# First attention scores as pairs of 64-row matmuls in six slots a step, with the turned maxima in a second-score bank

## The chip, the cores and the metric

The kernel runs on one core of a Trainium2 chip. Its time is the device time of one execution in microseconds (us); it is the median of several runs. The numbers of the profile come from one further execution that was recorded by the hardware profiler. Five engines work at once and meet only at semaphores: PE (TensorE, matmuls, with its weight loads shown apart as PEld), DVE (VectorE), ACT (ScalarE), POOL (GpSimd) and SP (SyncE, which here only issues DMAs).

## The reference, cut to what matters

The input is a batch of 8 sequences of 512 rows of 128 numbers. A modulated layer norm is followed by an attention block, its residual and a low-rank MLP, and then by a mixture of 8 experts with a shared expert. The change touches only the attention inside the first block:

```python
x = _layernorm(hidden_states, ln1_g, ln1_b)
Q = jnp.einsum('bsd,dhr,hre->bhse', x, q_U, q_V) + q_b[None, :, None, :]
K = ...
V = ...
scores = jnp.einsum('bhse,bhte->bhst', Q, K) * scale     # 16 heads of 8 numbers
scores = jnp.where(causal[None, None], scores, -1000000000.0)
attn = jax.nn.softmax(scores, axis=-1)
ctx = jnp.einsum('bhst,bhtd->bhsd', attn, V)
```

## The kernel before, in words

**What is multiplied.** A head has only 8 numbers a row, but they are wanted to near float32 precision. So Q and K are each split into three bf16 parts, and the six products of parts that matter (`PRODUCTS`) are stacked: 6 x 8 = 48 rows (`SROWS`) of contraction hold one head. Three more rows hold the negated maximum of each score row, again in three bf16 parts, against rows of ones on the side of K (`MROWS`, together `QROWS` = 51).

**Two passes over the scores.** The first scores (`s1`, L1232) have the queries on the partitions. DVE takes the maximum of each row of them (`take_max`, L1661, recorded at L1669). The second scores (`s2`, L1257) have the keys on the partitions and already contain the negated maximum, so ACT can take the exponential of them (`exp_unit`, L979, recorded at L989) and write the result where `context` (L1280, recorded at L1293) multiplies it with V. V has a column of ones, so that the sum of the exponentials comes with it.

**Steps and units.** A step handles one of 4 groups of 4 heads of one batch element: 32 steps (`NG`). In step n PE works on the second scores of n, on the context of n-1 and on the first scores of m = n+3. The first scores of a step are 12 units (`S1_UNITS`): two units for query tile 0 and two for query tile 1, each of two heads, and four units of one head each for tiles 2 and 3. The second scores are 6 units (`S2_UNITS`).

**How a unit is computed.** A first-score unit starts with one matmul of the causal mask (L1245, `ident_b` by `later_q`, over 128 rows), and then has one matmul a head (L1248). All of them contract over 128 partitions: `q_st` has a slice for each of the 4 heads in which the 64 partitions of the other half are zero, and `k_st` holds two heads above each other. The zeros are written once (ACT, L971, and two DMAs of zero rows in front, L534 to L538). A second-score unit works on 64-row halves instead: its two mask matmuls (L1272) and its score matmuls (L1276) alternate between partitions 0 to 63 and 64 to 127, each half with a PSUM bank of its own.

**The ring.** `ps_r` has three PSUM banks. `ring_order` (L115) lists everything that passes through them, in the order in which PE writes it: first-score units (S), the turned maxima (M), the transposed input (T), the projections Q, K and V, the output projection (O) and the transposed second norm (U). The entry at place k uses bank k mod 3, and `bank` (L1175) lets PE wait until the earlier entry in that bank has been read. `ps_s2` has four banks for the second scores, two for each unit in turn.

**The order on PE** (`step`, L1306): s2 units 0 and 1; context of key tile 0; s1 units 0 and 1; O; s1 2 and 3; s2 2 and 3; context of tiles 1 to 3; M; s1 4 and 5; T, K, V; s1 6 and 7; Q; s2 4 and 5; s1 8 to 11; U. T and Q come in one step of four, K and O in the next, V in the third and U in the fourth.

**The way of the maxima.** POOL splits the 16 maxima a row into bf16 parts (`split_max`, L825), PE turns them (`transpose_max`, L1252, recorded at L1254), ACT copies them to `max_rows` (`empty_max`, L1017, recorded at L1020), and SP stores them to DRAM (`store_max`, L592, recorded at L597) and loads them into the stack for the second scores two steps later (`load_max`, L599).

**Layer norms on DVE.** Between the maxima DVE does the norms of later and earlier batch elements: `layer_norm` (L1621) runs one half of a step's share after unit 3 and the other after unit 7. The batch elements' first norms end after about half of the steps; the second norms go on to the end.

**At the end.** In step 27 (`EARLY_STEP`) SP waits for several things and then issues the large loads for the MLP (L671 to L679); the loads and stores of the following steps stand behind them in its queue. `store_ctx` (L609) is one of these, and ACT's `empty_ctx` (L1022) waits for it two steps later.

Of the kernel before, what the change touches and what calls it, by code (L numbers as in the profile page):

```python
# [114 lines left out]
def ring_order():  # L115
# [12 lines left out]
    for n in range(FIRST_STEP, LAST_STEP + 1):  # L128
# [21 lines left out]
BY_ACT = {one: k for k, one in enumerate(one for one in RING if one[0] in "MTKVQU")}  # L150
# [95 lines left out]
def adaln_block(nc, a, out):  # L246

    ctx = ExitStack()
    with ctx:
# [6 lines left out]
        def sem(name):  # L256
            return ctx.enter_context(nc.semaphore(name))
# [35 lines left out]
        q_st = [first.take(GROUPS, JH, S, dt=BF16) for k in range(2)]  # L293
# [15 lines left out]
        q_d = dram("q_d", (2, len(PRODUCTS) + 1, P, S), BF16)  # L309
# [12 lines left out]
        def attend():  # L322
# [49 lines left out]
            later_q = sb("later_q", [P, P], BF16, until=front)  # L372
            ident_h = sb("ident_h", [P, HALF], BF16, until=front)
            lower_k = sb("lower_k", [P, P], BF16, until=front)
            upper_k = sb("upper_k", [P, P], BF16, until=front)
# [9 lines left out]
            consts, consts2, k_ones, v_ones, q_zeroed = sem("consts"), sem("consts2"), sem("k_ones"), sem("v_ones"), sem("q_zeroed")  # L385
# [8 lines left out]
            act_emptied, dve_emptied, zero_rows = sem("act_emptied"), sem("dve_emptied"), sem("zero_rows")  # L394
# [3 lines left out]
            max_split, max_stored, max_loaded = sem("max_split"), sem("max_stored"), [sem("max_loaded0"), sem("max_loaded1")]  # L398
# [6 lines left out]
            def ring(name, k):  # L405
                return ps_r[:, RING_BANK[PLACE[name, k]], :]

# [117 lines left out]
            with nc.Block() as block:  # L525
                @block.sync
                def _(sp):
# [6 lines left out]
                    sp.wait_ge(v_zeroed, 1)  # L534
                    for k in range(2):
                        sp.dma_start(q_d[k, len(PRODUCTS)].rearrange("p (c s) -> p c s", c=2),
                                     zeros[:].bitcast(BF16).unsqueeze(1).to_broadcast([P, 2, S // 2])).then_inc(zero_rows, 16)
# [14 lines left out]
                    def store_stack(b, m):  # L552
# [5 lines left out]
                        dst = (q_d, k_d)[m][b % 2, 0:len(PRODUCTS)].rearrange("k p s -> p k s")  # L558
# [11 lines left out]
                    def load_stack(b, g, of="qk"):  # L570
# [5 lines left out]
                        if b < 2:  # L576
                            wait(sp, k_ones, b + 1)
                            wait(sp, q_zeroed, b + 1)
                            wait(sp, zero_rows, 32)
# [1370 lines left out]
```

## Time and profile before

| | |
|---|---|
| median of 3 runs | 707.96 us (705.23 to 709.73) |
| the profiled execution | 706.39 us, of which the span from first to last instruction is 704.6 us |
| busy shares of the span | PE 90%, PEld 59%, DVE 64%, ACT 58%, POOL 43% |
| front part | first score matmul at 42.2 us |
| attention steps with first and second scores | 66 to 358 us |
| MLP, routing and experts | 382 us to the end |

"Busy" is the time in which at least one instruction of the engine was recorded as running. Matmuls overlap, and the end of a matmul is modelled, so a PE that is busy all the time may still be waiting for its own pipeline.

### The profile page before, as it was taken

To read this page: it belongs to the slowest core of one execution; us is meant where nothing else is said; L and a number is where in the kernel's file an instruction comes from. 1 tells how busy PE (TensorE), PEld (TensorE's weight loads), DVE (VectorE), ACT (ScalarE), POOL (GpSimd) and SP (SyncE) were. 2 spreads that over 40 slices of the span, in tenths; PEclk is the share of its full clock that TensorE was granted. 3 is DMA by queue.
4 is the path that set the end of the run, shared out by engine and by line. 5 is a ranking of instruction groups with operands and counts; after the bars stand their busy time and mean duration, and the time that the engine had idled before them with its cause. 6 is when DMAs were issued, how large, how long until landed. Compare 5 with 4: busy or idle time off the path is not lost.

```text
span 704.6 us, 15442 instructions
## 1 busy us (share of the span) xinstructions
PE 633.6 (90%) x5389; PEld 416.6 (59%) x5389; DVE 447.6 (64%) x1346; ACT 409.1 (58%) x720; POOL 301.7 (43%) x480
## 2 busy tenths in 40 slices
PE   4977899999999999999978886999998999999997
PEld 3543444444444544444434575766766999999993
DVE  5749887878788776767742878777673222222227
ACT  4432667676676767666666565676434555555550
POOL 4232424243442524232313438766771545455452
PEclk9999999999999999999999998999899999999999
DMA  9552332443343344332463511211236777777769
GB/s 212 189 177 74 118 102 87 144 138 113 109 153 102 126 140 136 131 106 72 132 189 108 143 36 50 81 51 50 70 96 197 205 239 222 221 224 225 234 209 322
DMA packets 86125, 100.97 MB, mean 143 GB/s; under 512 B 13008, under 2 KB 68216, under 8 KB 85952
## 3 DMA queue, kind: packets, MB, share of 16 engines
q1 hardware_dynamic: 76896, 87.19, 40.3%
q0 software_dynamic: 4544, 9.45, 3.7%
q10 hardware_dynamic: 4608, 3.35, 1.8%
q8 instruction: 43, 0.70, 0.4%
q14 instruction: 34, 0.28, 0.1%
HBM read 60.28 MB, written 37.57 MB: 139 GB/s over the span
## 4 chain that ended last, share of the span: by engine, by line
PE 53%; DVE 14%; DMA 9%; ACT 8%; SPq 6%; issue 5%; POOL 4%; POOLq 0%; ACTq 0%; DVEq 0%
PE ps_pv L1293 9%; PE ps_r L1478 7%; PE ps_s L1468 6%; DVE row_max L1669 6%; PE ps_r L1248 5%; PE ps_r L1245 4%; DMA arena<-slots_d 4%; PE ps_pv L1364 4%; PE ps_s L1276 3%; POOL slots_d L910 3%; PE ps_r L1223 2%; PE ps_s L1272 2%; PE ps_s L1372 2%; ACT arena L1081 2%; DMA arena<-in_w_mod 1%
## 5 line engine op out<-in xcount | busy, mean ns | idle before, releaser
L1669 DVE TENSOR_REDUCE row_max<-ps_r 128x1 f32<-128x384 f32 (+3 forms) x384 | 206.9, 595 | 63.1 <-PE ps_r L1248 61.8
L989 ACT ACTIVATE arena<-ps_s 128x1024 f32<-128x1024 f32 (+1 forms) x192 | 159.3, 881 | 70.8 <-PE ps_s L1276 69.8
L1248 PE MATMUL ps_r<-arena 128*128 128x384 bf16 (+3 forms) x512 | 118.7, 303 | 0.0
L956 POOL DMA_INDIRECT y_d<-arena,target x78 | 74.9, 960 | 87.7 <-DVE arena L1878 75.5
L1245 PE MATMUL ps_r<-later_q,ident_b 128*128 128x128 bf16 (+1 forms) x384 | 91.4, 244 | 22.0 <-DVE row_max L1669 15.8
L1245 PEld LDWEIGHTS ps_r<-later_q,ident_b 128*128 128x128 bf16 x384 | 35.9, 97 | 84.1 <-DVE row_max L1669 42.4
L1874 DVE TENSOR_TENSOR arena<-ps_r,arena_early 128x256 f32<-128x256 f32 x39 | 16.6, 425 | 108.2 <-PE ps_r L1478 108.2
L1293 PE MATMUL ps_pv<-arena 128*32 128x512 f32 (+3 forms) x1024 | 83.3, 443 | 0.1
L910 POOL DMA_INDIRECT slots_d<-arena,slots x64 | 65.5, 1023 | 18.2 <-issue 18.2
L1276 PE MATMUL ps_s<-arena 51*128 51x256 bf16 (+3 forms) x512 | 59.9, 298 | 0.0
L1478 PEld LDWEIGHTS ps_r<-arena 128*128 128x128 f32 x480 | 58.2, 192 | 1.5
L1144 ACT ACTIVATE arena<-ps_s,arena 128x256 f32<-128x256 f32 x120 | 50.4, 471 | 13.9 <-PE ps_s L1468 13.2
L1478 PE MATMUL ps_r<-arena 128*128 128x128 f32 x480 | 58.3, 275 | 0.0
L1248 PEld LDWEIGHTS ps_r<-arena 128*128 128x128 bf16 x512 | 50.6, 99 | 12.8 <-issue 2.4
L1468 PE MATMUL ps_s<-arena 128*128 128x256 f32 x240 | 56.8, 379 | 0.0
L831 POOL TENSOR_SCALAR neg_part<-row_max 128x16 bf16<-128x16 f32 x32 | 8.3, 260 | 89.0 <-DVE row_max L1669 89.0
L1293 PEld LDWEIGHTS ps_pv<-arena 128*32 128x32 f32 x1024 | 27.0, 110 | 32.2 <-issue 25.8
L1468 PEld LDWEIGHTS ps_s<-arena 128*128 128x128 f32 x240 | 43.3, 190 | 4.6
L1272 PE MATMUL ps_s<-ident_h,lower_k 64*128 64x64 bf16 (+1 forms) x384 | 39.9, 204 | 5.2 <-ACT arena L989 4.7
L1102 ACT ACTIVATE arena<-ps_s,cols 128x512 f32<-128x512 f32 x32 | 21.6, 686 | 31.6 <-PE ps_s L1372 30.9
L770 POOL TENSOR_TENSOR var_eps<-moments,ln_eps 128x4 f32<-128x4 f32 x24 | 4.9, 203 | 79.9 <-DVE moments L1494 79.9
L1272 PE MATMUL ps_s<-ident_h,upper_k 64*128 64x64 bf16 (+1 forms) x384 | 38.7, 198 | 0.0
(236 smaller groups left out, 1129.1 us busy)
## 6 DMA issues: line engine op xcount, KB each, us to landing
arena<-in_ew SPq DMA_DIRECT2D x30, 514.0 KB
ctx_d<-ctx_raw SPq DMA_DIRECT2D x32, 256.0 KB, 3.1
arena<-q_d SPq DMA_DIRECT2D x64, 102.0 KB
arena<-k_d SPq DMA_DIRECT2D x64, 96.0 KB
arena<-slots_d SPq DMA_DIRECT2D x39, 132.0 KB, 3.1
arena_early<-in_ew SPq DMA_DIRECT2D x9, 514.0 KB
arena<-y_d SPq DMA_DIRECT2D x8, 512.0 KB, 6.0
q_d<-arena_early SPq DMA_DIRECT2D x8, 384.0 KB, 2.9
```

Of the source, the lines that this page charges most:

```text
L910: pool.indirect_dma_start(slots_d[:], bass.IndirectOffsetOnAxis(ap=slots[:, c, i:i + 1], axis=0), n3x[:, c, i, :], None).then_inc(scattere ...
L956: pool.indirect_dma_start(y_d[:], bass.IndirectOffsetOnAxis(ap=target[:, k, c:c + 1], axis=0), res[:, k, c, :], None).then_inc(put[k], 16)
L989: act.activation(dst, src, ACT.Exp, scale=SCALE).then_inc(exp_done, 1)
L1144: act.activation(x_hidden[:, k, f], ps_s2[:, 2 * (k % 2) + f // 2, (f % 2) * SLOTS:(f % 2 + 1) * SLOTS], ACT.Relu, bias=x_w[k][:, FF + NF ...
L1245: pe.matmul(diag, ident_b[:], later_q[:].unsqueeze(1).to_broadcast([P, len(js), P]), start=True, stop=False, skip_group_check=True)
L1248: mm = pe.matmul(bnk[:, k * keys:(k + 1) * keys], q_st[b % 2][:, g, j, i * P:(i + 1) * P], k_st[b % 2][:, g, j // 2, 0:keys], start=False, ...
L1272: pe.matmul(banks[half][:, :, at:at + HALF], stationary[whole], near, start=(at == 0), stop=False, skip_group_check=True)
L1276: mm = pe.matmul(banks[j % 2][:, k // 2, :], k_st[b % 2][rows, g, j // 2, kt * P:(kt + 1) * P], q_st[b % 2][rows, g, j, kt * P:S], start=F ...
L1293: mm = pe.matmul(ps_pv[32 * j:32 * j + 32, kt * P:S], v_sb[b % 2][:, kt, GROUPS * j + g, :], probs[:, p % 2, at:at + length], start=(kt == ...
L1468: mm = pe.matmul(ps_s2[:, 2 * (k % 2) + f // 2, (f % 2) * SLOTS:(f % 2 + 1) * SLOTS], x_w[k][:, f * P:(f + 1) * P], tok_t[:, k], start=Tru ...
L1478: mm = pe.matmul(ps_s1[:, k % 2, c * P:(c + 1) * P], x_hidden[:, k, f, c * P:(c + 1) * P], x_w[k][:, FF + f * D:FF + (f + 1) * D], start=( ...
L1669: dve.reduce_max(row_max[:, m % 2, js[0] % 2, j:j + len(js), i], src, AXIS.X).then_inc(max_taken, 1)
```

## The change

The first scores are computed like the second ones. `q_st` loses the zero halves (two slices a group, not four), and a pair of units, one for each 64-row half, is written together into two ring banks: first the mask matmuls of both halves, two to a half (`lower_q`, `upper_q`, 64 columns a head each), then the score matmuls, alternating between the halves. PE waits for both banks before it starts the pair. The zero rows, their DMAs and ACT's two fills of `q_st` go. The order of the step is written anew in six slots, each with one pair of first-score units and one second-score unit; the context is cut into four, O moves behind the second half of the step. The turned maxima leave the ring: they are written to columns 384 to 447 of bank 3 of `ps_s2`, which only second-score unit 1 uses. ACT still copies them behind the exponential of unit 3, which itself comes later in the step, and units 1 and 5 of the second scores wait for that copy. DVE's norms are cut into quarters, after units 1, 3, 7 and 9.

```diff
@@ ring_order
-        units(m, 0, 1)
-        one(n, "O")
-        units(m, 2, 3)
-        if 0 <= m - 1 < NG:
-            order.append(("M", m - 1))
-        units(m, 4, 5)
-        one(n, "T", "K", "V")
+        units(m, 0, 1, 2, 3, 4, 5)
+        one(n, "T", "K")
         units(m, 6, 7)
+        one(n, "O", "V")
+        units(m, 8, 9)
         one(n, "Q")
-        units(m, 8, 9, 10, 11)
+        units(m, 10, 11)
@@ s1
-        for u in units:
+        for u in units[::2]:
...
+            banks = [bank("S", NS1 * m + u + half)[:, 0:len(js) * keys].rearrange(...) for half in range(2)]
+            for stationary, at in ((lower_q, keys - P), (upper_q, keys - HALF)):
+                for half in range(2):
+                    whole = slice(HALF * half, HALF * half + HALF)
+                    near = ident_h[whole].unsqueeze(1).to_broadcast([HALF, len(js), HALF])
+                    pe.matmul(banks[half][:, :, at:at + HALF], stationary[whole], near, start=(at == keys - P), stop=False, ...)
             for k, j in enumerate(js):
+                for half in range(2):
+                    rows = slice(HALF * half, HALF * half + SROWS)
+                    mm = pe.matmul(banks[half][:, k, :], q_st[b % 2][rows, g, j // 2, i * P:(i + 1) * P],
+                                   k_st[b % 2][rows, g, j // 2, 0:keys], start=False, stop=True, ...)
+                    if k == len(js) - 1:
+                        mm.then_inc(s1_done, 1)
@@ transpose_max
         pe.wait_ge(max_split, SPLIT_OPS * (m + 1))
+        wait(pe, max_copied, m)
+        wait(pe, exp_done, NS2 * n + 2)
+        pe.transpose(max_turned(), ...)
@@ s2
+        if u == 1:
+            wait(pe, max_copied, min(n + LAG - 1, NG))
+        if u == 5:
+            wait(pe, max_copied, min(n + LAG, NG))
@@ step on PE, new order
+        s1(m, 0, 1)
         s2(n, 0)
+        context(n - 1, 0)
+        s1(m, 2, 3)
         s2(n, 1)
+        context(n - 1, 1)
+        s1(m, 4, 5)
         s2(n, 2)
+        context(n - 1, 2)
+        context(n - 1, 3)
         (T, K where due)
+        s1(m, 6, 7)
+        transpose_max(n)
+        s2(n, 3)
+        (O, V where due)
+        s1(m, 8, 9)
+        s2(n, 4)
         (Q where due)
+        s1(m, 10, 11)
+        s2(n, 5)
         (U where due)
@@ step on ACT
         exp_unit(n, 2)
-        exp_unit(n, 3)
-        empty_max(n + LAG - 1)
         empty_ctx(n - 1)
-        qk_middle(b, 0)
         empty_t, empty_qk(b, 1)
+        exp_unit(n, 3)
+        empty_max(n + LAG - 1)
         empty_v
+        qk_middle(b, 0)
+        exp_unit(n, 4)
         empty_qk(.., 0)
-        exp_unit(n, 4)
         exp_unit(n, 5)
@@ layer_norm on DVE
-        second = u == 7
+        second = u > 4
+        quarters = {1: (0, 1), 3: (2, 3), 7: (0, 1), 9: (2, 3)}[u]
```

The masks on POOL become two tensors of 192 columns instead of three of 128.

## Rows read from the trace of the kernel before

**Rows 1.** The page: the chain that ended last, by engine.

```profile
PE 53%; DVE 14%; DMA 9%; ACT 8%; SPq 6%; issue 5%; POOL 4%; POOLq 0%; ACTq 0%; DVEq 0%
```

**Rows 2.** Windows of four steps, an early and a late batch: busy us, clock, DMA.

```profile
172.30:213.77 41.47, 38.60 (x434) 19.48 (x432) 34.16 (x90) 28.28 (x42) 16.70 (x33) 1.00 0.38 128
...
255.22:296.70 41.48, 39.11 (x438) 19.70 (x436) 29.75 (x64) 28.68 (x42) 14.24 (x29) 1.00 0.38 128
```

**Rows 3.** Chain of waits, first-score units: start us, us, what.

```profile
98.46 0.11 PE ps_r L1245
98.57 0.11 PE ps_r L1248 x2
...
98.79 0.22 PE ps_r L1248 x2
...
101.96 0.06 PE ps_r L1245
102.01 0.16 PE ps_r L1248
...
105.86 0.22 PE ps_r L1248
```

**Rows 4.** Chain of waits, second-score units on 64-row halves.

```profile
96.86 0.06 PE ps_s L1272 x4
96.92 0.22 PE ps_s L1276 x2
...
99.81 0.06 PE ps_s L1272 x4
99.87 0.16 PE ps_s L1276 x2
...
104.98 0.22 PE ps_s L1276 x4
105.21 0.11 PE ps_s L1272 x4
105.32 0.11 PE ps_s L1276 x4
```

**Rows 5.** Chain of waits, what else PE does in a step.

```profile
97.13 0.99 PE ps_pv L1293 x8
...
100.03 1.43 PE ps_pv L1293 x24
...
102.17 0.55 PE ps_r L1209 x4
...
103.67 1.10 PE ps_r L1223 x2
```

**Rows 6.** Timeline of DVE and PE: start us, us, instruction, idle before it.

```profile
231.34 0.76 DVE L1669 TENSOR_REDUCE row_max<-ps_r 128x2 f32<-128x256 f32 x2 [1.01 <-PE ps_r L1248]
...
231.36 1.11 PE L1303 MATMUL ps_r<-w_out,ctx_n 128*128 128x128 f32 x8
...
232.83 1.29 DVE L1669 TENSOR_REDUCE row_max<-ps_r 128x2 f32<-128x512 f32 x2 [0.74 <-PE ps_r L1248]
...
245.38 1.02 DVE L1669 TENSOR_REDUCE row_max<-ps_r 128x1 f32<-128x384 f32 x2 [0.26 <-PE ps_r L1248]
...
251.72 1.96 DVE L1669 TENSOR_REDUCE row_max<-ps_r 128x2 f32<-128x256 f32 x4 [0.73 <-PE ps_r L1248]
```

**Rows 7.** Chain of waits behind step 27: SP's queue and a store.

```profile
348.42 5.38 SPq L673
...
358.45 4.73 DMA ctx_d<-ctx_raw
```

**Rows 8.** Windows of 2 us in the first steps: busy us, granted clock.

```profile
52.00:54.00 2.00, 0.90 (x6) 0.42 (x6) 1.93 (x9) 0.00 (x0) 1.04 (x4) 1.00 0.00 1
...
56.00:58.00 2.00, 1.94 (x9) 0.83 (x9) 1.85 (x5) 0.00 (x0) 0.00 (x0) 0.50 0.41 139
...
60.00:62.00 2.00, 1.33 (x11) 0.63 (x9) 2.00 (x6) 0.00 (x0) 0.90 (x4) 1.00 0.19 67
```

**Rows 9.** Timeline of ACT in the front part, behind its fills of the stacks.

```profile
21.57 0.78 ACT L996 ACTIVATE arena_early<-ps_r,cols 128x512 f32<-128x512 f32 x1 [8.43 <-PE ps_r L1209]
```

More of the change, by code:

```diff
@@ L289, in adaln_block @@
         work = first.take(2 * PT_LEN)
-        q_st = [first.take(GROUPS, JH, S, dt=BF16) for k in range(2)]
+        q_st = [first.take(GROUPS, 2, S, dt=BF16) for k in range(2)]
+        first.at += GROUPS * 2 * S
         k_st = [first.take(GROUPS, 2, S, dt=BF16) for k in range(2)]
@@ L606, in load_max @@
                             row = HALF * half + SROWS
[L607 removed]
+                            sp.dma_start(q_st[b % 2][row:row + MROWS, g], src[:, half]).then_inc(max_loaded[m % 2], 16)
                     def store_ctx(p):
@@ L1252, in transpose_max @@
-                    def transpose_max(m):
+                            banks = [bank("S", NS1 * m + u + half)[:, 0:len(js) * keys].rearrange("p (j s) -> p j s", s=keys) for half in range(2)]
+                            for stationary, at in ((lower_q, keys - P), (upper_q, keys - HALF)):
+                                for half in range(2):
+                                    whole = slice(HALF * half, HALF * half + HALF)
+                                    near = ident_h[whole].unsqueeze(1).to_broadcast([HALF, len(js), HALF])
+                                    pe.matmul(banks[half][:, :, at:at + HALF], stationary[whole], near, start=(at == keys - P), stop=False,
+                                              skip_group_check=True)
@@ L1632, in layer_norm @@
                         if b is not None:
-                            for i in range(NT):
+                            for i in quarters:
                                 if second:
@@ L1639, in layer_norm @@
                         if b is not None:
-                            for i in range(NT):
+                            for i in quarters:
                                 if second:
@@ L1646, in layer_norm @@
                         if b is not None:
-                            for i in (2, 3) if second else (0, 1):
-                                normalise(b, i)
+                            normalise(b, quarters[0] // 2 + 2 * second)
                         b = batch_at(n, AFTER_STATS_AT)
                         if b is not None:
-                            for i in range(NT):
+                            for i in quarters:
                                 if second:
@@ L1657, in layer_norm @@
                         if b is not None:
-                            for i in (2, 3) if second else (0, 1):
-                                normalise_after(b, i)
+                            normalise_after(b, quarters[0] // 2 + 2 * second)
                     def take_max(m, u):
```

109 lines of the change are left out of this document (43 added, 66 removed).

## The prediction

> **What bounds the kernel now.** I read the chain by engine first: PE carries 53% of it and DVE 14% [rows 1], so the end is set by PE with DVE in between. Then the windows of four steps. In the attention a batch of four steps takes 41.47 us with PE busy 38.60, DVE 34.16 and ACT 28.28; in a late batch, when the first norms are over, the length is the same with DVE at 29.75 [rows 2]. So PE is nearly full, and DVE is second with 7.3 us of idle time a batch (41.47 - 34.16), 11.7 late. Last the timeline: DVE's waits, 0.3 to 1.0 us each, are for first scores [rows 6]. They come because PE goes off for second scores and context (0.99 us for key tile 0, 1.43 us for the rest [rows 5]) while the ring holds only three units of DVE work. The change touches both: it takes work from PE, and it spreads first-score units over the step.
>
> **PE's saving.** A first-score unit costs, by its pitch in the chain: tile 0: 0.11 + 0.11 = 0.22; tile 1: 0.11 + 0.22 = 0.33; tile 2: 0.06 + 0.16 = 0.22; tile 3: 0.06 + 0.22 = 0.28 [rows 3]. A step has 2, 2, 4 and 4 of them: 0.44 + 0.66 + 0.88 + 1.12 = 3.1 us. A new pair has the form of a present second-score unit, column for column: four masks of 64 columns in 0.06 and two matmuls of 512 in 0.22 or of 384 in 0.16; four masks of 128 in 0.11, four matmuls of 128 in 0.11 or of 256 in 0.22 [rows 4]. So a pair costs 0.22, 0.33, 0.22 or 0.28, and a step has 1, 1, 2, 2 of these: 1.55 us. Saved: 1.55 us a step, 6.2 a batch. Changes between array shapes: context of tile 0 takes 0.99 us [rows 5] for 4 x 512 columns in 0.85, so a change costs about 0.1; plain steps have eight both before and after, and O, V and Q now sit between 64-row neighbours, 0.6 us more a batch. PE's work a batch falls from about 38.6 to 33 busy, or 31.3 by pitch: four plain steps of 6.3 (below) and 6.1 for projections and transposes (T 0.55, U alike, K, Q, V, O 1.1 each [rows 5, 6], with their changes of shape).
>
> **What DVE then allows.** DVE's work does not shrink. In pairs the maxima cost 0.76 (tile 0), 1.29 (512 columns) or 1.02 (384) [rows 6]: 0.76 + 1.29 + 2 x 1.02 + 2 x 1.29 = 6.67 us a step, 26.7 a batch. Today four tile-0 and tile-1 units run on in 1.96 [rows 6], slightly better than 2.05; the groups broken up cost 1.0 a batch in all. The rest of 34.16 is 8.5 us of norms. New floor by DVE: 35.2 us a batch, 30.7 late. Both floors lie far under 41.5; what counts is how the two engines mesh. I go slot by slot. A pair needs two of three banks, so PE may start it when DVE has taken the first unit of the pair before, and needs about 0.05 for the semaphore, 0.17 for the pipeline to fill, and the pair itself. Between two deliveries PE has:
> - to slot 2 (tile 1): second-score unit, context 0, change, pair: 0.28 + 0.99 + 0.11 + 0.33 = 1.71 us;
> - to slot 3: 0.28 + 0.75 + 0.11 + 0.22 = 1.36; to slot 4: 0.22 + 0.75 + 0.11 + 0.22 = 1.30; to slot 5: M 0.27, 0.33, 0.28 = 0.88; to slot 6: 0.61; to the next slot 1: 0.44 (together 6.3).
> DVE has 0.76, 1.29, 1.02, 1.02, 1.29, 1.29 there and a quarter of the norms after slots 1, 2, 4 and 5. In an early batch (norm quarters of 0.3 to 0.7) DVE idles:
> - step with V: slot 2 comes 0.16 late, V (1.1) makes slot 5 0.25 late: 0.4;
> - step with U: 0.1; U itself fits while PE waits, but as an odd entry in a ring of three it makes the next pair wait for both units before it: the next step loses 0.4 there and 0.4 at slot 2, and T (0.55) makes slot 4 0.5 late: 1.3;
> - step with K and O: 0.44 at slot 2, 1.1 at slot 4 (K before the pair), and 0.65 in which DVE waits for O itself: 2.2.
> Sum 4.1, so a batch takes 35.2 + 4.1 = 39.3, a gain of 2.1 us. In a late batch the same slots with smaller quarters idle 1.3 + 0.5 + 2.8 + 2.7 = 7.3: 30.7 + 7.3 = 38.0, a gain of 3.5. There are some 4.5 early and 2.5 late batches with both kinds of scores: 9.5 + 8.7 = 18.2 us.
>
> **A rule on evacuation, and one on modes.** The row shows DVE busy 34.16 of 41.47 us [rows 2] before PE gets any faster. The Trainium skill (TensorEngine Tiling (Array Packing), PSUM Bottleneck) says that tiling speeds up the matmuls but not the reading of PSUM, which may become the bottleneck; it speaks against counting PE's 6.2 us a batch as the gain. By the rule at its strictest a batch would be DVE's 35.2; by the slots it is 39.3. The same page (Key Properties) has a change of tiling mode drain the array; the 0.1 us in the context's 0.99 [rows 5] agrees.
>
> **What is moved, and its price.**
> - The turned maxima. Counted from the step's second-score unit 0, they are turned about 4.8 us into a step today (four second-score units 1.1, context 0.99 + 1.43, four first-score units 1.1, M 0.17 [rows 3 to 5]). Now M stands as late after slot 1 (1.71 + 1.36 + 1.30 and its own 0.3), and ACT copies behind the exponential of unit 3 (0.8, with 0.3 of matmuls and 0.3 of latency): 1.2 us later. Behind it in ACT's queue stand V's emptying, a cast and exponential 4, which has over 1 us of slack, and in SP's queue `store_ctx` and the loads of later stacks, which have a step or more. In the middle this costs nothing: the maxima are wanted more than a step later, and the new waits of units 1 and 5 are for a copy long done or 1 us old. If a step's cover is gone, each costs the 1.2 us. It does cost once: in step 27 SP's long loads stand behind `load_max`; one of them is held 5.38 us, and ACT then waits for a store of 4.73 us [rows 7]. That chain starts with M of step 27, so gains behind it are lost (left out of the 7 batches above) and the 1.2 us is paid. Lower end 0 (SP is held by something else), upper end 3.
> - The clock. In the first steps, before second scores begin, PE waits for DVE already. The clock fell to its lower level, 1.2 GHz (0.50 in 56 to 58 us), after PE had been busy 0.90 of 2 us; with 1.33 of 2 us it held [rows 8]. With half the work in the first scores those steps (some 25 us) will run at the lower level. A pair then takes 0.44 to 0.66, more than DVE's second unit leaves, 0.15 us in each of 18 slots: 2.5 us lost. Lower end 0, upper end 5.
> - The front part: two fills on ACT and two DMAs fewer. ACT idles 8.43 us behind its fills before the first transposed input comes [rows 9], so they are hidden and their going brings nothing; at most 1 us through lighter DMA. The masks on POOL are 7 + 6 instructions instead of 9 + 7, with about as many elements; they are hidden behind PE's 6.9 us of small products. Loads of `q_st` move 48 rows instead of 51: nothing.
>
> **Sum.** 706.4 (span 704.6 and 1.8 around it) - 18.2 + 1.2 + 2.5 = 691.9 us. The median of the runs shown is 1.6 us above the profiled execution, so I forecast 693.5 us.
>
> **The rivals.**
> 1. DVE becomes the one bound and the slots mesh better than I think. For it: DVE's waits need only 0.3 us more of lead at slot 2. Against it: K, O and T still stand ahead of a pair. If half of the idle time I count (2 us early, 3.6 late) goes, 4.5 x 2 + 2.5 x 3.6 = 18 us more: 676.
> 2. The mesh is no better than now: pairs need two banks of three, and DVE keeps its 7.3 us of idle a batch on a work 1.0 us larger: 42.5 early. Late, with 10 idle, 40.7. That is 4.5 x 1.0 - 2.5 x 0.8 = +2.5, and 3.7 for maxima and clock: 714; halfway between this and my forecast, 704. For it: three banks, PE blocked in order. Against it: waits today come from runs of four units ahead of 2.4 us of other work, which the slots end.
> 3. The clock falls inside the steps (other side). Between slot 4 and the next slot 1 PE has 1.9 us of work in 4.3 us of DVE's. With filled pipelines that shows as about 65% busy, near the 1.33 of 2 that held, above the 0.90 that fell [rows 8]. If it falls, the work there is hidden, but context 0 and slots 2 and 3 run at half speed: 1.71 + 1.36 = 3.1 us more. In one step of four, seven times, that is 22 us: 715. It decides from five such falls on (15 us); in every step it would be over 760.
> 4. The halves don't run side by side, so the change doesn't do what it says: PE stays at 3.1 us a step and only the order changes, with 0.6 us a batch for changes of shape and the 3.7: 706.4 + 4.2 + 3.7 + 1.6 = 716. Against it stand the second scores, where two 512-column matmuls take 0.22 [rows 4].
>
> **How the numbers follow.** Chances: forecast 0.55, rival 1 0.13, rival 2 0.18, rival 3 0.12, rival 4 0.02. The forecast's own range is 684 to 701 (costs at their ends, and 1 us a batch either way). The range for 8 in 10 leaves out about half of rival 1 and most of rival 3: 677 to 709. A measurement of this kernel can tell about 1%, 7 us, from no change. Faster by over 1% (below 701): forecast nearly whole and rival 1: 0.67. Within 1%: 0.18, rival 2 above all. Slower: 0.15, from rivals 3, 2 and 4.
>
> **What would show it.** In the profile after: L1245's and L1248's successors with twice the matmuls and some 1.5 us less of pitch a step; a window of four early steps of about 39.3 us with DVE busy near 35 and PE near 33; DVE's longest waits at slot 4 of the K step and at O; the clock at 0.5 between 50 and 70 us and at 1.00 from the first second scores on; SP's 5.38 us stall still there, and the wait after it as long or longer. Wrong would be: a batch of 41 us or more (meshing), one under 37 (rival 1), a clock under 0.95 in the steady windows (rival 3), or second-score units waiting for ACT's copy of the maxima.

## The result and the profile after

The changed kernel takes 726.27 us (median of 4 runs, 724.77 to 730.82) against 708.17 us of the kernel before, run beside it (4 runs, 705.23 to 709.73): ratio 1.0271, 95% interval 1.0215 to 1.0328. It is slower; the forecast of 693.5 us and its range, 677 to 709, are missed, on the far side. One further execution, of 738.74 us, was in a slower state and is left out. The profiled execution took 730.82 us with a span of 729.1; that of before took 706.39, 24.4 us less.

The page of the kernel after: busy times, granted clock by slices, and the chain by engine.

```profile
PE 605.4 (83%) x5773; PEld 391.1 (54%) x5773; DVE 450.6 (62%) x1346; ACT 411.5 (56%) x718; POOL 301.5 (41%) x478
...
PEclk9855599999998798999997999899999999999999
...
PE 50%; DVE 15%; DMA 12%; SPq 8%; ACT 7%; issue 5%; POOL 3%; ACTq 0%; POOLq 0%; DVEq 0%
```

PE's share of the chain falls from 53% to 50% [rows 1], so the change took work from the engine that bounded the kernel, and the time went up all the same. The three fives in the clock row are the first steps; in two later slices it stands at 7.

To see where, I cut both attention parts at the start of the first maximum of every fourth step (m = 0, 4, ..., 28) and at the end of the last maximum: the window's length is then DVE's own pitch, and doesn't depend on where a marker stands in PE's order. Windows of the kernel before, then of the kernel after (length, busy us of PE, PEld, DVE, ACT, POOL, granted clock, DMA share, GB/s):

```profile
42.66:79.76 37.10, 27.67 (x194) 13.15 (x193) 31.80 (x74) 14.56 (x23) 12.86 (x27) 0.91 0.38 125
79.76:119.08 39.32, 37.14 (x423) 17.96 (x422) 32.04 (x84) 27.65 (x41) 14.22 (x31) 1.00 0.32 105
119.08:158.99 39.91, 37.98 (x431) 18.99 (x430) 32.01 (x78) 27.59 (x41) 14.24 (x30) 1.00 0.37 125
158.99:200.44 41.45, 38.58 (x435) 19.48 (x434) 34.16 (x91) 28.25 (x42) 16.70 (x34) 1.00 0.38 126
200.44:241.88 41.44, 38.57 (x435) 19.45 (x434) 34.07 (x90) 28.25 (x42) 16.68 (x33) 1.00 0.38 128
241.88:283.06 41.18, 38.58 (x435) 19.47 (x434) 29.96 (x66) 28.25 (x42) 14.24 (x29) 1.00 0.39 128
283.06:321.29 38.23, 35.90 (x427) 18.50 (x426) 28.82 (x63) 24.14 (x35) 10.82 (x27) 1.00 0.34 117
321.29:358.30 37.01, 34.87 (x421) 18.03 (x419) 28.72 (x63) 23.39 (x34) 9.21 (x23) 1.00 0.42 129
```

```profile
43.33:85.42 42.09, 25.79 (x225) 11.95 (x225) 32.56 (x74) 12.71 (x21) 11.97 (x24) 0.58 0.31 98
85.42:125.08 39.66, 33.77 (x474) 15.33 (x468) 32.07 (x84) 28.10 (x39) 12.45 (x29) 0.93 0.25 80
125.08:168.53 43.45, 35.20 (x482) 16.55 (x476) 32.13 (x79) 29.31 (x41) 15.63 (x33) 0.92 0.38 123
168.53:210.39 41.86, 32.87 (x485) 16.08 (x480) 34.11 (x92) 29.52 (x42) 16.81 (x34) 1.00 0.38 125
210.39:260.08 49.69, 39.85 (x485) 17.80 (x480) 36.38 (x91) 29.62 (x42) 16.76 (x34) 0.83 0.33 105
260.08:303.27 43.19, 35.26 (x485) 16.61 (x480) 30.36 (x68) 29.50 (x42) 14.57 (x30) 0.92 0.37 120
303.27:341.86 38.59, 31.43 (x477) 15.32 (x472) 29.30 (x64) 25.54 (x35) 10.80 (x26) 0.96 0.41 134
341.86:378.52 36.66, 30.64 (x477) 14.87 (x472) 29.23 (x64) 25.89 (x35) 9.73 (x25) 1.00 0.36 106
```

The differences are +5.0, +0.3, +3.5, +0.4, +8.2, +2.0, +0.4 and -0.4 us, 19.6 in all; 0.7 us had been lost ahead of them. From the last maximum to the last addition of an output projection it takes 43.9 us before and 49.1 after; the MLP and the experts behind it take what they took (302.4 and 301.5 us).

Two things can be read here. In the one early batch that stands wholly at clock 1.00 (41.86 us), PE's busy time did fall, from 38.6 to 32.9, but PE idles 9.0 us (2.9 before) and DVE 7.8 (7.3 before): the time that PE won became waiting. That batch is 0.4 us longer than before and 2.6 us longer than the forecast's 39.3, with no help from the clock. And the batches that lose more are those with a low clock. The granted clock has two levels, 1.2 and 2.4 GHz, so 43.45 us at 0.92, 49.69 at 0.83 and 43.19 at 0.92 hold about 7, 17 and 7 us at the lower one. At half speed PE's work there can be late by half of that at most, 3.5, 8.5 and 3.5 us (an estimate); lost against before are 3.5, 8.2 and 2.0.

The pairs themselves do what the change says. The chain of after, near step 28 (start us, us, what):

```profile
352.12 0.22 PE ps_r L1240 x4
352.34 0.22 PE ps_r L1245 x4
...
353.62 0.16 PE ps_r L1240 x4
353.78 0.17 PE ps_r L1245 x2
```

A pair's score matmuls, four of 256 columns or two of 384, take 0.22 and 0.17 us; that is the forecast's price from [rows 4]. The masks ahead of them, 0.22 and 0.16, hold the 0.1 us for the change of shape behind the context. Rival 4 is out.

The waits inside the batch at full clock, 168.53 to 210.39 us, and the first one behind it. Timeline of DVE in the kernel after (in brackets: idle before, and what ended it), and two rows of PE from the same stretch:

```profile
187.13 0.55 DVE L1699 RECIPROCAL recs<-sums 128x64 f32<-128x64 f32 x1 [0.81 <-DMA sums<-ctx_d]
...
191.37 1.29 DVE L1676 TENSOR_REDUCE row_max<-ps_r 128x2 f32<-128x512 f32 x2 [1.31 <-PE ps_r L1245]
...
204.82 1.02 DVE L1676 TENSOR_REDUCE row_max<-ps_r 128x1 f32<-128x384 f32 x2 [1.19 <-PE ps_r L1245]
207.07 0.69 DVE L1692 TENSOR_TENSOR h_sb<-ps_r,h_sb 128x512 f32<-128x512 f32 x1 [1.23 <-PE ps_r L1310]
...
213.40 1.29 DVE L1676 TENSOR_REDUCE row_max<-ps_r 128x2 f32<-128x512 f32 x2 [1.61 <-PE ps_r L1245]
```

```profile
190.83 0.28 PE L1240 MATMUL ps_r<-ident_h,later_q 64*128 64x128 bf16 x4 [0.79 <-ACT after_t L1021]
...
205.91 1.13 PE L1310 MATMUL ps_r<-w_out,ctx_n 128*128 128x128 f32 x8 [0.62 <-ACT arena_early L996]
```

Row by row: the wait for the sums of the probabilities, whose load stands behind the stack loads in SP's queue; slot 2 behind U, where PE waits until ACT, busy with the first exponential, has emptied U; slot 4 behind K, the 1.1 us of the forecast; O, which PE can't start before ACT has emptied K's bank; and slot 2 again in a step where the clock is low. Windows of 2 us around that fall:

```profile
208.00:210.00 2.00, 0.71 (x16) 0.56 (x18) 2.00 (x6) 1.46 (x3) 1.92 (x4) 1.00 0.36 126
210.00:212.00 2.00, 2.00 (x22) 0.54 (x22) 1.79 (x6) 1.50 (x2) 1.67 (x5) 0.60 1.08 391
212.00:214.00 2.00, 2.00 (x22) 0.86 (x22) 0.60 (x1) 0.06 (x1) 1.37 (x2) 0.54 0.10 26
```

PE had waited for DVE, busy 0.71 of 2 us, and then the clock stands at its lower level, 1.2 GHz, for about 3.4 us in these two windows. The context of key tile 0, 0.99 us [rows 5], takes 1.93 there. This is rival 3's picture. Counted over the trace between 100 and 360 us, the clock is low for 34 us, where before it was low for none. What this costs the kernel as a whole is less certain: the experiments below raise the clock and win little.

The end: from the chain of after, and then PE's wait there in the timeline of before and of after:

```profile
371.26 4.87 SPq L669
...
381.32 5.11 DMA ctx_d<-ctx_raw
...
389.72 1.86 PE ps_pv L1300 x8
```

```profile
364.92 0.20 PE L1272 MATMUL ps_s<-ident_h,lower_k 64*128 64x64 bf16 x2 [2.83 <-ACT arena L989]
```

```profile
388.10 0.40 PE L1279 MATMUL ps_s<-ident_h,later_k 64*128 64x128 bf16 x4 [6.28 <-ACT max_rows L1011]
```

SP's stall and ACT's wait for a store are still there, about as long as in [rows 7]. But in the new order of ACT exponential 3 and the copy of the maxima stand behind `empty_ctx`, which is what waits for that store, and second-score unit 5 waits for the copy: PE stands for 6.28 us where it stood for 2.83. This is the one place where second scores wait long for the copy, a sign of being wrong that the prediction named. The context behind it runs at the low clock. I did not test this part by itself.

### The profile page after: what moved, and what is told of

The parts are those of the page before. It is cut to its first block, busy times and chain, and to the rows that moved or that the text cites. A ratio compares the mean times of both kernels' runs of the same rounds, so it can differ in the third digit from the quotient of the medians.

```text
span 729.1 us, 16417 instructions
## 1 busy us (share of the span) xinstructions
PE 605.4 (83%) x5773; PEld 391.1 (54%) x5773; DVE 450.6 (62%) x1346; ACT 411.5 (56%) x718; POOL 301.5 (41%) x478
## 3 DMA queue, kind: packets, MB, share of 16 engines
q1 hardware_dynamic: 76608, 86.53, 39.7%
## 4 chain that ended last, share of the span: by engine, by line
PE 50%; DVE 15%; DMA 12%; SPq 8%; ACT 7%; issue 5%; POOL 3%; ACTq 0%; POOLq 0%; DVEq 0%
PE ps_pv L1300 9%; DVE row_max L1676 8%; PE ps_r L1486 7%; PE ps_s L1476 7%; PE ps_r L1240 4%; PE ps_pv L1372 4%; PE ps_r L1245 3%; DMA arena<-slots_d 3%; POOL slots_d L904 3%; PE ps_s L1283 3%; DMA k_d<-arena_early 2%; DMA arena<-y_d 2%; PE ps_r L1216 2%; PE ps_s L1380 2%; SPq L585 2%
## 5 line engine op out<-in xcount | busy, mean ns | idle before, releaser
L1676 DVE TENSOR_REDUCE row_max<-ps_r 128x1 f32<-128x384 f32 (+3 forms) x384 | 212.0, 594 | 67.2 <-PE ps_r L1245 65.0
L980 ACT ACTIVATE arena<-ps_s 128x1024 f32<-128x1024 f32 (+1 forms) x192 | 168.3, 882 | 96.6 <-PE ps_s L1283 94.3
L1240 PEld LDWEIGHTS ps_r<-ident_h,later_q 64*128 64x128 bf16 x768 | 25.3, 96 | 156.4 <-DVE row_max L1676 78.3
L1240 PE MATMUL ps_r<-ident_h,later_q 64*128 64x64 bf16 (+1 forms) x768 | 51.3, 212 | 67.3 <-DVE row_max L1676 63.5
L1300 PE MATMUL ps_pv<-arena 128*32 128x512 f32 (+3 forms) x1024 | 99.3, 487 | 0.0
L1245 PE MATMUL ps_r<-arena 48*128 48x384 bf16 (+3 forms) x512 | 75.6, 329 | 0.0
L904 POOL DMA_INDIRECT slots_d<-arena,slots x64 | 66.1, 1034 | 18.2 <-issue 17.9
L1283 PE MATMUL ps_s<-arena 51*128 51x256 bf16 (+3 forms) x512 | 72.3, 315 | 0.0
L1279 PE MATMUL ps_s<-ident_h,later_k 64*128 64x64 bf16 (+1 forms) x768 | 49.9, 206 | 8.1 <-ACT max_rows L1011 6.3
L1279 PEld LDWEIGHTS ps_s<-ident_h,later_k 64*128 64x128 bf16 x768 | 37.1, 100 | 26.8 <-ACT arena L980 12.5
L851 POOL TENSOR_TENSOR ctx_n<-ctx_t,rec_rows 128x512 f32<-128x512 f32 x8 | 10.4, 1298 | 60.7 <-DMA rec_rows<-rec_d 60.6
```

Of the source, the lines that this page charges most:

```text
L904: pool.indirect_dma_start(slots_d[:], bass.IndirectOffsetOnAxis(ap=slots[:, c, i:i + 1], axis=0), n3x[:, c, i, :], None).then_inc(scattere ...
L980: act.activation(dst, src, ACT.Exp, scale=SCALE).then_inc(exp_done, 1)
L1240: pe.matmul(banks[half][:, :, at:at + HALF], stationary[whole], near, start=(at == keys - P), stop=False, skip_group_check=True)
L1245: mm = pe.matmul(banks[half][:, k, :], q_st[b % 2][rows, g, j // 2, i * P:(i + 1) * P], k_st[b % 2][rows, g, j // 2, 0:keys], start=False, ...
L1279: pe.matmul(banks[half][:, :, at:at + HALF], stationary[whole], near, start=(at == 0), stop=False, skip_group_check=True)
L1283: mm = pe.matmul(banks[j % 2][:, k // 2, :], k_st[b % 2][rows, g, j // 2, kt * P:(kt + 1) * P], q_st[b % 2][rows, g, j // 2, kt * P:S], st ...
```

## The experiments

Each kernel was timed beside runs of the kernel before on the same chip. On the chips used the kernel before takes 708 to 724 us, so only ratios are compared. The chips differ behind the attention: in the traces of the changed kernel on two of them (after and after_again) the last addition of an output projection ends at 427.6 and 428.6 us, and what follows takes 301.5 and 318.2. The sixteen kernels went in four groups.

### First group: the two halves of the change, filler, and two waits

**order_only**: the new order, the cut norms and the free corner, with the first scores as before.

```diff
-banks = [bank("S", ...) for half in range(2)]   # masks and scores, alternating
+bnk = bank("S", n)                               # one mask over 128 rows, then the scores
```

> The new order of the step, ACT's and DVE's new orders and the turned maxima in the corner, but first scores as before: one unit at a time over 128 rows. Mesh theory (the new order and the single entries in a ring of three cost the time): about as slow as the change or slower, 720 to 735, since PE has 1.55 us more a step and the same waits behind O, U and T. Clock theory (the time is lost because half-empty PE lets the clock fall): PE keeps its columns, the granted clock stays at 0.97 or more in the span, and the time comes back to 705 to 713.

Measured: ratio 1.0516 (1.0449 to 1.0583), clock 0.951: slower than either theory had it.

**pairs_only**: pairs in the old order, the maxima in the ring.

> First scores in pairs of 64-row halves, in the old order of the step with the maxima in the ring. Mesh theory: the pairs alone do little harm, since the singles stand where they stood: 700 to 712. Clock theory: PE has the same few columns as in the change, so the clock falls in the first steps and now and then later (0.92 to 0.96 over the span), and the time is 715 to 728.

Measured: 1.0500 (1.0432 to 1.0568), clock 0.914. Again slower than either theory had it. Neither half is a gain: each alone costs 5%, both together 2.5 to 2.7%. That the order needs the time that the pairs free is my reading of this; which waits make the pairs in the old order slow was not traced down (its clock is low for 51 us between 100 and 360).

**fill_steps**: the change, with idle mask rounds ahead of the second scores, so that PE has more to do. Each round is started and then overwritten by the unit's own masks.

```diff
+FILL_S2 = {3: 4, 4: 6, 5: 8}
+for _ in range(FILL_S2.get(u, 0)):
+    for half in range(2):
+        pe.matmul(banks[half][:, :, 0:HALF], lower_k[half], near, start=True, stop=False)
```

> The change, with 18 further rounds of mask matmuls a step ahead of second-score units 3, 4 and 5 (0.85 us of PE at the full clock), which are overwritten by the real masks: work that brings nothing but fills PE where it waits for DVE. Clock theory: from the first second scores on the clock is back at 0.98 to 1.00, and the time falls by 4 to 12 us, to 714 to 722. Mesh theory: PE waits there anyway, so the time stays within 3 us of the change's 726, or rises.

Measured: 1.0245 (1.0177 to 1.0313), about the changed kernel's own ratio (1.0271, and 1.0251 in the second group; it was not run on this chip). The low clock between 100 and 360 us fell from 34 to 14 us, and the median did not follow: 4 to 12 us were expected of the clock.

**singles**: the change, with O and V behind units 8 and 9 (slot 6; ACT empties V behind exponential 4), and U emptied at the end of its own step.

```diff
-one(n, "O", "V")
 units(m, 8, 9)
+one(n, "O", "V")
...
-exp_unit(n, 0); empty_after(...)      # first thing of the next step
+qk_middle(b, 1); empty_after(...)     # end of the same step
```

> The change, with O and V moved one slot on, between the second-score unit 4 and the last pair, where DVE has most to do, and the transposed second norm (U) emptied by ACT at the end of its own step instead of behind the first exponential of the next. Mesh theory: DVE's waits at O (1.2 us) and behind U (0.8 to 1.3 us) go, some 2 us a batch, 12 to 16 us in all: 710 to 716. Clock theory: little, 722 to 727.

Measured: 1.0196 (1.0110 to 1.0283). Of the 12 to 16 us expected some 4 came, within the intervals. The waits for O went (in the traces 6.0 us in all before the edit, 0.2 with it), those for the sums did not (6.6 and 8.4 us).

### Second group: the waits mended, and filler everywhere

**after_again** is the changed kernel itself on the second group's chip.

> The changed kernel itself, beside the following ones on the same chip: 1.027 times the time of before if the first measurement carries over; the granted clock low for some 25 to 30 us in the first steps and for 30 to 50 us later.

Measured: 1.0251 (1.0189 to 1.0313), the first measurement over again.

**fill_all**: as fill_steps, with 22 rounds a step, and 512-column matmuls ahead of each pair in the first three steps.

> The change, with idle matmuls in both places where PE waits for DVE: two of 512 columns ahead of each pair in the three steps before the second scores, and 22 rounds of mask matmuls a step ahead of second-score units 3, 4 and 5. Clock theory: the low clock in the first steps (some 30 us) and later (34 us of the attention) goes, and 8 to 14 us come back: ratio 1.008 to 1.016. Mesh theory: little of it comes back, ratio 1.02 to 1.03, since DVE idles behind ACT, the sums and O and not for PE's work.

Measured: 1.0175 (1.0104 to 1.0245), clock 0.953: between the two theories, and its interval overlaps that of after_again.

**waits**: singles, and the loads of the sums ahead of the loads of the stacks in SP's queue.

```diff
+load_ctx(batch_at(n, CTX_AT))
 for g, later in ((0, 0), (1, 0), (2, 1), (3, 2)):
     ...                               # loads of the stacks
-load_ctx(batch_at(n, CTX_AT))
```

> The change with three waits moved away: O and V one slot later, U emptied by ACT at the end of its own step, and the loads of the sums ahead of the stacks in SP's queue. No filler. Mesh theory: DVE's waits at O (1.2 us) and for the sums (1.3 us) go, 2.5 us a batch, 15 to 18 us in all: ratio near 1.005. Clock theory: PE's idle stretches stay as long, the clock falls as often or oftener, and the ratio stays between 1.015 and 1.03.

Measured: 1.0069 (1.0030 to 1.0108). The three lone waits together (O and V, U, the sums) were worth 1.8%, some 13 us, the largest part of the loss that an experiment isolates. The clock stayed: between 100 and 360 us it is low for 31 us in this trace, against 34 in after.

**waits_fill**: both.

> Both at once. If the two causes add up, 20 to 28 us come back: ratio 0.985 to 1.0. If the clock alone counts, as in fill_all. If neither is the cause, near 1.025.

Measured: 1.0058 (1.0026 to 1.0090); the 0.985 to 1.0 did not come. In the trace the filler does what the clock theory says; a batch of waits, and one of waits_fill:

```profile
168.83:213.20 44.37, 35.83 (x485) 16.71 (x480) 36.64 (x91) 29.51 (x42) 16.86 (x33) 0.92 0.35 118
```

```profile
163.72:203.98 40.26, 36.67 (x661) 19.85 (x656) 34.47 (x92) 29.28 (x42) 16.71 (x34) 1.00 0.40 130
```

4.1 us less in the same order, with the clock at 1.00. (The first of them holds some 7 us at the lower level, which can make PE's work late by 3.5 us at most, so not all of the 4.1 need be the clock.) But the medians are 728.40 and 727.08: filler in the whole kernel gives 0.1%, within its interval nothing. It takes PE's time itself, and falls of the clock remain elsewhere (a batch of 44.29 us at 0.92). So the low clock is real and goes with longer batches, but filler doesn't buy the time back.

### Third group: is it the coupling of the two banks?

A pair asks for two of three banks, and delivers both its units together. **apart** is waits with the two 64-row units of a pair issued one after the other, each behind its own bank, wherever the entry ahead of the pair is T, K, V, O, Q or U; **apart_all** does so for all pairs.

```diff
-banks = [bank("S", k0 + half) for half in range(2)]
-for ... in masks:  for half in range(2): pe.matmul(...)
-for k, j in ...:   for half in range(2): pe.matmul(...)
+for half in range(2):
+    banks[half] = bank("S", k0 + half)
+    for ... in masks: pe.matmul(...)
+    for k, j in ...:  pe.matmul(...)
```

> The kernel waits with one edit: where the ring's entry just ahead of a pair of first-score units belongs to T, K, V, O, Q or U (six pairs a batch of 24), the two 64-row units are issued one after the other, each behind its own bank, instead of interleaved behind both banks. Theory of the coupled banks (a pair asks for two of three banks at once, so behind a lone entry VectorE has nothing left to take while TensorE makes the pair): VectorE's idle time ahead of such pairs falls by some 0.3 to 0.5 us a time, 2 to 3 us a batch at most, and the ratio to the kernel before goes from waits' 1.007 to 0.990 to 1.000. Rival: the halves one after the other take longer, and the late unit is what decides; then it stays at 1.005 to 1.015, with VectorE idle only moved from the first unit of the pair to the second. Third theory, the clock: nothing here fills TensorE, so a ratio of 1.005 whatever the idle time inside.

Measured: 1.0029 (1.0002 to 1.0056), between the first theory's range and the others'.

> As apart, but all six pairs of a step are issued one unit after the other: 64-row units with nothing side by side, in the new order, with the waits mended. It measures what the side-by-side halves are worth in this order. By the forecast's price of the pairing (1.55 us of matrix work saved a step, some of it idle anyway) it is slower than waits by 0.5 to 1 us a step where TensorE's queue decides: ratio 1.02 to 1.04. If the pair's coupling costs as much as it saves, it equals waits, 1.00 to 1.012.

Measured: 0.9938 (0.9911 to 0.9964), 703.90 us against 708.19. Giving up the side-by-side issue altogether, for which the change was made, makes this kernel faster than the kernel before. The expectation of 1.02 to 1.04 failed outright.

**before_sums** is the kernel before with the loads of the sums first.

> The kernel before with one edit: the loads of the sums of probabilities go ahead of the loads of the stacks in the queue of SyncE, as in waits. In the kernel before the wait for the sums is 0.44 us a batch, so by the theory that this wait was the change's own harm it gives at most 0.5 us a batch, 3 us in all: ratio 0.996 to 1.000. If it gives 1 per cent or more, the sums' place was a fault of both kernels, and what waits won by it doesn't speak of the change.

Measured: 1.0039 (1.0013 to 1.0066). In the old order that edit is a small loss, a little outside the expected range (in the trace of before the waits for the sums are 0.43, 0.89, 0, 0.81 and 0.29 us), so the sums' place is no fault of both kernels.

**apart_fill**: apart, with the filler of waits_fill.

> apart with the idle matrix work of waits_fill (two 512-column matmuls ahead of each pair in the first three steps, 22 rounds of masks a step ahead of the second scores 3 to 5). If the clock is what remains once the waits are gone, the ratio is 0.985 to 0.995 and below apart's by 0.005 or more; if the filler costs as much as the clock gives back, as it did for waits, the ratio equals apart's within 0.004.

Measured: 1.0000 (0.9977 to 1.0024), so the filler costs about what it gives back. Its profile is the cleanest of the new order. A batch, then DVE's waits in it:

```profile
198.70:238.38 39.68, 37.02 (x661) 20.15 (x656) 34.39 (x92) 29.43 (x42) 16.66 (x34) 1.00 0.41 132
```

```profile
222.93 1.02 DVE L1690 TENSOR_REDUCE row_max<-ps_r 128x1 f32<-128x384 f32 x2 [0.57 <-PE ps_r L1254]
...
233.15 1.02 DVE L1690 TENSOR_REDUCE row_max<-ps_r 128x1 f32<-128x384 f32 x2 [1.18 <-PE ps_r L1254]
...
236.39 0.69 DVE L1706 TENSOR_TENSOR h_sb<-ps_r,h_sb 128x512 f32<-128x512 f32 x1 [0.47 <-PE ps_r L1324]
```

39.7 us a batch, 1.8 below the 41.45 of before. The forecast had 39.3, with 0.5 at slot 4 behind T, 1.1 behind K and 0.65 at O. Where the clock holds and the lone entries are out of the way, the slot-by-slot sum was right to 0.4 us for an early batch. Some of that is luck: DVE is busy for 34.4 and idle for 5.3 us, where the forecast had 35.2 and 4.1, and the two errors cancel.

### Fourth group: the change as it stands, and the order without halves

**after_apart**: the changed kernel, nothing mended, with the pairs issued apart.

> The changed kernel with one edit: the two 64-row units of a pair are issued one after the other, each behind its own bank. Nothing else is undone: the order, the loads, the masks by halves and the free corner stay. Theory of the coupled banks: the interleaving costs about as much here as it did with the mended waits (1.003 or 1.007 to 0.994, some 1 per cent), so the ratio falls from 1.025 to 1.010 to 1.018. Rival: TensorE's queue decides in this kernel because its waits stand in it, so the lost side-by-side time (some 1.5 us a step of matrix work by the forecast) comes back in full where it isn't idle; then 1.025 or more.

Measured: 1.0159 (1.0106 to 1.0212). The interleaving costs about 0.9% here (against after_again, measured on another chip; the intervals touch).

**apart_all_fill**: apart_all with the filler.

> apart_all with the idle matrix work of waits_fill (512-column matmuls ahead of the first-score units in the first three steps, 22 rounds of masks a step ahead of the second scores 3 to 5). apart_all still shows 31 us at the low clock between 100 and 360 us. If the clock is what is left, the ratio falls below apart_all's 0.994, to 0.982 to 0.990; if filler costs what it brings (as in the pairs of waits and waits_fill, and near that in apart and apart_fill), 0.990 to 0.998; if TensorE's queue is by now the bound, it rises above 1.000.

Measured: 0.9983 (0.9953 to 1.0014); filler does not help apart_all (the two were measured on different chips).

**order_waits**: order_only with the waits mended.

> The new order, the mended waits (O and V behind units 8 and 9, the turned U emptied at the end of its own step, the loads of the sums first) and the maxima in the free corner, but the first scores as before: 128 rows with a single mask, one unit after the other. It differs from order_only (1.052) by the mended waits alone and from apart_all (0.994) by the 128-row units and the eight unit loads of q. If the new order with clean waits is the gain, it equals apart_all within 0.005. If order_only's 1.05 came from something that the 128-row form brings into this order (its q stack loads, its mask), it stays at 1.02 or more.

Measured: 1.0269 (1.0204 to 1.0334). A batch of it at full clock, and one wait inside it, of ACT and of PE:

```profile
165.31:210.09 44.78, 40.04 (x434) 19.01 (x434) 34.51 (x91) 29.34 (x42) 16.72 (x34) 1.00 0.35 117
```

```profile
192.91 0.60 ACT L1025 ACTIVATE ctx_raw<-ps_pv 128x512 f32<-128x512 f32 x1 [2.63 <-DMA ctx_d<-ctx_raw]
...
194.24 0.50 PE L1247 MATMUL ps_r<-later_q,ident_b 128*128 128x128 bf16 x2 [2.50 <-ACT arena_early L996]
```

So the new order alone is no gain: with 128-row units a batch is 3.3 us longer than before. With halves, at full clock, it is 39.7 (apart_fill), 5.1 us shorter. Not all of this is the halves' matrix work. Once in the batch PE waits 2.50 us for a bank that ACT has not emptied, because ACT waits 2.63 us for the store of an earlier context; the waits of PE for ACT in the batch of apart_fill sum to 0.6 us. Why that store is late here (this kernel also loads larger stacks) was not tested.

**waits_again** repeats waits on this chip.

> The kernel of waits once more, on the chip of this job, so that apart_all's kind and the coupled kind are compared in one place: 1.004 to 1.010 by its first measurement. If it comes out near 0.995, then the difference between waits and apart_all was one of chips and not of the interleaving.

Measured: 1.0085 (1.0048 to 1.0122), as at first. apart_all was not run on this chip, but apart_all_fill was, 1.0% below waits_again; so the step from waits to apart_all, some 1.4%, is hardly one of chips.

### Where the coupling hurts

The first steps show it without second scores in between. Chain of the kernel after, from 59 to 63 us:

```profile
59.30 0.29 PE ps_r L1240 x4
59.59 0.44 PE ps_r L1245 x2
60.04 0.69 DVE row_max L1676
60.73 0.14 issue
60.86 0.29 PE ps_r L1240 x4
```

It is a closed loop: DVE takes the first unit of a pair (0.69), which frees the second bank that the next pair needs; 0.14 for the semaphore; the next pair at the low clock, 0.29 + 0.44 = 0.73. That makes 1.56 us, and DVE has 1.29 us of work in it, so it idles 0.27 in each. The same pair at full clock, from a later stretch of the same trace:

```profile
340.13 0.23 PE ps_r L1240 x4
340.36 0.25 PE ps_r L1245 x2
340.61 0.69 DVE row_max L1676
```

Here the pair takes 0.48 from its first mask to DVE's start, and the loop 0.69 + 0.14 + 0.48 = 1.31 us, against DVE's 1.29: DVE is hardly late, but there is no room left. Apart, the first unit is there sooner and the second one is made while DVE reads. The first four steps of waits (coupled), apart_all (apart) and apart_fill (mostly coupled, with filler):

```profile
43.39:85.85 42.46, 27.04 (x225) 12.36 (x225) 32.61 (x73) 12.84 (x21) 11.99 (x24) 0.50 0.30 97
```

```profile
43.75:81.92 38.17, 32.16 (x223) 16.16 (x224) 31.77 (x73) 12.82 (x21) 12.04 (x23) 0.50 0.33 105
```

```profile
43.06:77.77 34.71, 26.47 (x303) 11.59 (x302) 31.96 (x73) 11.96 (x20) 12.12 (x23) 1.00 0.34 104
```

Coupled at the low level these steps take 42.5 us, apart at the low level 38.2, and mostly coupled at the full level 34.7 (37.1 before, at 0.91). Coupling and the low clock each have a price, and the coupling's is paid where the clock is low: 4.3 us in these four steps alone. The changed kernel and after_apart take 42.09 and 38.35 us there, 3.7 us apart, about half of what separates them in all. At full clock no price of the coupling shows: an early batch takes 39.7 us in apart_fill and 39.6 to 39.8 in apart_all_fill.

## Why the prediction was wrong, point by point

- **What bounds the kernel, and PE's saving**: right. A pair costs what a second-score unit costs, and PE's busy time a batch fell to 32.9 us at full clock, as forecast (33).
- **The slots: this is the step that failed.** The sum gave DVE 4.1 us of idle time in an early batch and so 39.3 us; the batch of the changed kernel at full clock has 7.8 us of it and takes 41.86. I gave U 0.4 us at slot 2 and O 0.65. U's bank is emptied by ACT only behind the first exponential, so slot 2 came 1.31 late; and O waits for the emptying of K, which I had not named, so it came 1.23 late. The wait for the sums of the probabilities was not in the forecast at all. In the batch shown it is no longer than before (0.81 against 0.89 us), but over the attention up to the last maximum it grows from 2.4 to 6.6 us in five batches. Slot 4 behind K was right (1.19 against 1.1). With the smaller repetitions of these the mended waits are worth 1.8% (after_again to waits). I had counted what PE and DVE do in a slot, and not who empties each lone entry and what stands ahead in that engine's queue. Where those entries were out of the way and the clock held, the batch was 39.7.
- **The 18.2 us** had a second fault. It takes 3.5 us from each of 2.5 late batches of 41.5 us, but of the last three only one is so long (41.18, then 38.23 and 37.01). Even with the waits mended the gains there are 0.9, 1.3 and 1.7 us (waits: 40.27, 36.90, 35.32 us), 3.9 in place of 8.7.
- **"The clock in the first steps, 2.5 us, upper end 5"**: the mechanism was right, the size was not: 5.0 us by the windows. I took the pair at the low clock as 0.44 to 0.66 and it was 0.63 to 0.85; and it was compared with DVE's second unit without the semaphore, which takes 0.14 where I had 0.05. The closed loop gives 0.27 a pair, not 0.15.
- **The clock inside the steps, which the sum put at nothing (rival 3, given 0.12)**: it fell, and was at the low level for 34 us between 100 and 360 us. The argument against it was an average over the rest of a step ("about 65% busy"); the fall shown came in the step of K and O, where PE was busy 0.71 of 2 us. It is tempting to say that the missed waits above fed it, but mending them left 31 us at the low level (waits) and 27 (waits_again). What keeps the clock falling there is not shown.
- **Rival 2, the mesh no better than now**: 714 us, 12 short of the measured time, by a cause close to a part of it: the batch at full clock is no shorter than before, with DVE as idle as before. Its half-sentence "pairs need two banks of three" is what after_apart and apart_all show: about 0.9% with the waits in place, 1.4% with them mended.
- **Rival 1** is out: DVE idles 7.8 us in the batch at full clock, against 7.3 before. The rule of the Trainium skill (TensorEngine Tiling (Array Packing), PSUM Bottleneck), that tiling speeds up the matmuls and not the reading of PSUM, warned in the right direction; here, with DVE busy 34.11 of 41.86 us, it was not DVE's rate that took the gain but the hand-over of banks between the engines.
- **The maxima and the tail**: in the steps between 100 and 360 us the second scores never stood for ACT's copy, as forecast. Behind the last maximum 5.2 us were lost where I had 1.2 (upper end 3), with PE's 6.28 us for the copy behind ACT's wait for the store. I had asked where M stands in PE's order, and not that the copy would stand behind `empty_ctx`; untested.

Step by step, mending the waits and issuing the pairs apart bring the 2.5% to -0.6%: those two account for the kernel being slower than before, and not for all of the 2% that the forecast had it faster. What the low clock costs by itself stays open: batches that hold some 7 us of it are 2 to 4 us longer than their like without, but filler moved the medians by 0.8% (change), 0.1% (waits) and 0.3% (apart), and against apart_all by -0.4%, on another chip.

## What to carry to other kernels

Before matmuls are interleaved so that two units finish together, look at the ring that takes them: a pair that needs two of three buffers ties PE to the reader's first unit, and the loop "reader's first unit, semaphore, whole pair" must stay under the reader's two units at the lower clock as well (here 1.31 us at full clock and 1.56 at the low one, against 1.29). Price every lone entry of such a ring by who empties it and what stands ahead in that engine's queue. Do the same for what is moved in another engine's order: a copy put behind a wait for a store inherits that wait. And when PE is freed from work while another engine sets the pace, compute the time at the lower clock too, and don't argue a fall away by an average.

## What the runs showed of the hardware that was not expected

- The record of the granted clock can begin late, and a stretch without a record reads as 1.00. In the trace of after_apart it begins at 85.9 us (in that of after at 26.1), so its first four steps, 43.64 to 81.99 us, read 1.00, although the two 512-column float32 matmuls of a projection at 66.4 us take 1222 and 1061 ns, as in the kernel after (1220 and 1061 at 69.2 us), where the record says 1.2 GHz; in apart_fill they take 697 and 592 at 64.9 us, where it says 2.4. The duration of a matmul that appears in all kernels is the safer reading.
- Matmuls on one 64-row half without a partner were no loss: apart_all, whose halves are never interleaved, beat its interleaved sibling by 1.4%. In this order 64-row units one after the other (ratio 0.994) also beat 128-row units (1.027), whose stacks are half zeros; of that a part is ACT's wait for a store, above.
- The clock fell behind a stretch of 2 us in which PE was busy for 0.71, with no single wait of PE over 0.9 us in it (0.89 and 0.65), and then stood at the lower level for about 3.4 us although PE was busy throughout.
